# Weighing the values of four attention heads in one block instead of four: exponentials double-buffered by group

## The reference, cut to what matters

```python
Q = (query @ Wq.T + bq)      # per head 128 x 32
K = (key_value @ Wk.T + bk)  # per head 2048 x 32
V = (key_value @ Wv.T + bv)
scores = jnp.einsum('bhqd,bhkd->bhqk', Q, K) / scale
weights = jax.nn.softmax(scores, axis=-1)
attn = jnp.einsum('bhqk,bhkd->bhqd', weights, V)
```

## Time and profile before

| | |
|---|---|
| device time, median of 3 runs | 2168.75 us (2167.66 to 2169.62) |
| the profiled execution, its own time | 2168.71 us |
| its span in the trace | 2166.6 us |
| PE busy in the span | 1995.5 us, 92% |
| DVE, ACT, POOL busy | 1440.0, 858.5, 1177.4 us |
| mean granted clock of PE | 0.959 of full speed |
| attention, first scores to last multiplication | 145.5 to 1240.3 us of the span |

### The profile page before, as it was taken

One profiled execution on the slowest core, in us unless ns is written; L12 is line 12 of the kernel. 1 busy time (PEld: TensorE's weight loads), 2 busy tenths in 40 slices (PEclk: granted clock), 3 DMA queues, 4 the chain that ended last, 5 costly groups with the idle time before them and its releaser, 6 DMA issues. The chain is left out here.

```text
span 2166.6 us, 41731 instructions
## 1 busy us (share of the span) xinstructions
PE 1995.5 (92%) x15544; PEld 1422.7 (66%) x15544; DVE 1440.0 (66%) x1442; ACT 858.5 (40%) x1239; POOL 1177.4 (54%) x837
## 2 busy tenths in 40 slices
PE   6989999999999999999955579989999999899999
PEld 3867777777777777777744338655555554378874
DVE  5126766767676767667665458089999995836555
ACT  1124444444444444444422214276676651133310
POOL 3126667676666766666644431079989993322200
PEclk9999999999999999999975689999999999999999
DMA  4545555555555555555422150040040003001101
GB/s 176 152 137 170 161 178 173 154 179 170 163 168 162 174 174 161 169 166 168 144 87 67 37 182 0 16 104 1 1 117 1 1 16 127 20 6 68 53 1 39
DMA packets 181602, 229.57 MB, mean 106 GB/s; under 512 B 21312, under 2 KB 111936, under 8 KB 175264
## 3 DMA queue, kind: packets, MB, share of 16 engines
q1 hardware_dynamic: 181408, 226.91, 34.0%
HBM read 153.30 MB, written 73.53 MB: 105 GB/s over the span
## 5 line engine op out<-in xcount | busy, mean ns | idle before, releaser
L368 POOL TENSOR_TENSOR a_half<-a_pt 128x1024 f32<-128x1024 f32 x128 | 306.9, 2398 | 373.9 <-ACT a_pt L418 373.9
L418 ACT ACTIVATE a_pt<-a_shift 128x2048 f32<-128x2048 f32 x128 | 245.1, 1915 | 555.7 <-PE a_o L600 460.3
L487 DVE TENSOR_TENSOR a_shift<-a_s,a_neg_rows 128x2048 f32<-128x2048 f32 x128 | 293.3, 2291 | 195.7 <-ACT a_neg_rows L430 195.7
L474 DVE TENSOR_REDUCE a_top<-a_s 128x128 f32<-128x2048 f32 x128 | 293.1, 2290 | 73.7 <-PE a_s L575 73.7
L575 PE MATMUL a_s<-a_q_stack,a_stack 32*128 32x128 f32 x4096 | 163.9, 301 | 48.0 <-DVE a_shift L487 40.2
L575 PEld LDWEIGHTS a_s<-a_q_stack,a_stack 32*128 32x128 f32 x4096 | 138.6, 202 | 93.0 <-DVE a_shift L487 72.8
L534 PE MATMUL a_pj<-p_c_hi,p_wk_hi 128*128 128x512 f32 x448 | 198.5, 443 | 0.0
L963 POOL TENSOR_TENSOR s_even_drive<-s_du,l_rows 128x512 f32<-128x512 f32 x128 | 162.7, 1271 | 64.3 <-DMA s_c_row<-bc_scratch 61.1
L359 POOL TENSOR_TENSOR p_c_lo<-a_raw,p_c_hi 128x512 fp32r<-128x512 f32 x120 | 153.0, 1275 | 73.9 <-ACT p_c_hi L405 73.9
L534 PE MATMUL a_pj<-p_wv_hi,p_c_hi 128*128 128x512 f32 x448 | 185.4, 414 | 0.0
L971 POOL TENSOR_TENSOR s_odd_seen<-s_odd_state,s_c_row 128x512 f32<-128x512 f32 x128 | 162.7, 1271 | 34.0 <-DVE s_odd_state L1102 15.1
(11 more groups left out here) (206 smaller groups left out, 3819.3 us busy)
## 6 DMA issues: line engine op xcount, KB each, us to landing
kv_scratch<-a_k_new SPq DMA_DIRECT2D x128, 256.0 KB, 2.5
kv_scratch<-a_v_new SPq DMA_DIRECT2D x128, 256.0 KB, 3.6
a_stack<-kv_scratch SPq DMA_DIRECT2D x512, 64.0 KB, 2.3
a_v<-kv_scratch SPq DMA_DIRECT2D x32, 1024.0 KB, 6.4
a_raw<-in_ctx SPq DMA_DIRECT2D x120, 256.0 KB, 3.4
a_q_stack<-q_scratch SPq DMA_DIRECT2D x128, 64.0 KB, 2.1
s_c_row<-bc_scratch SPq DMA_DIRECT2D x32, 256.0 KB, 6.0
e_ew_raw<-in_ew SPq DMA_DIRECT2D x8, 1024.0 KB, 4.9
```

What stands on the lines that cost most here:

```text
L368: nc.gpsimd.tensor_tensor(half[:], w[:, 0:2], w[:, 2:4], ALU.add).then_inc(halved, 1)
L418: nc.scalar.activation(pt_head(g, p), shift[:].rearrange("p (i n) -> p i n", n=BANK), ACT.Exp).then_inc(exped, 1)
L474: dve.tensor_reduce(top[:], s_ps[:].rearrange("p i n -> p (i n)").rearrange("p (k q) -> p q k", q=L), AX.X, ALU.max).then_inc(blocked, 1)
L487: dve.tensor_tensor(shift[:].rearrange("p (k q) -> p k q", q=L), s_ps[:].rearrange("p i n -> p (i n)").rearrange("p (k q) -> p k q", q=L), ...
```

## The change

`pt` becomes twice as large, with one half for even and one for odd groups, always head first. The exponentials of group g now wait only until group g - 2 has been weighed and halved (and the first two groups for nothing). PE weighs all four chunks of group g - 1 together in slot 1 of group g, 64 matmuls in a row, and sums the parts in slot 2, by the new function `total`. Slots 0 and 3 weigh nothing. The number of matmuls, their shapes, and all other engines' lists are the same. `finish_group` stays after the shift of slot 3.

```diff
-        pt = st.sb("pt", [P, HG, CH, BANK])
+        pt = st.sb("pt", [P, 2, HG, CH, BANK])
...
-        pt_head = lambda g, p: pt[:, p] if g % 2 == 0 else pt[:, :, p]
-        pt_chunk = lambda g, p, i: pt[:, p, i] if g % 2 == 0 else pt[:, i, p]
+        pt_head = lambda g, p: pt[:, g % 2, p]
+        pt_chunk = lambda g, p, i: pt[:, g % 2, p, i]
...
-                if not (fresh and g == 0):
-                    act.wait_ge(weighed, CH * (GROUPS * b + g - 1) + p + 1)
-                    act.wait_ge(halved, HG * (GROUPS * b + g))
+                if not (fresh and g <= 1):
+                    act.wait_ge(weighed, CH * (GROUPS * b + g - 1))
+                    act.wait_ge(halved, HG * (GROUPS * b + g - 1))
...
-            def weigh(b, g, i, fresh):
+            def weigh(b, g, fresh):
-                if i == 0:
-                    pe.wait_ge(exped, HG * (GROUPS * b + g + 1))
-                    pe.wait_ge(v_in[g % 2], 16 * (GROUPS // 2 * b + g // 2 + 1))
-                    if not (fresh and g == 0):
-                        pe.wait_ge(out_ready, GROUPS * b + g)
-                for j in range(KV):
+                pe.wait_ge(exped, HG * (GROUPS * b + g + 1))
+                pe.wait_ge(v_in[g % 2], 16 * (GROUPS // 2 * b + g // 2 + 1))
+                if not (fresh and g == 0):
+                    pe.wait_ge(out_ready, GROUPS * b + g)
+                for i in range(CH):
+                    for j in range(KV):
...
+                    mm.then_inc(weighed, 1)
+            def total(b, g):
+                pe.wait_ge(parted, HG * (GROUPS * b + g + 1))
...
-                if g >= 1:
-                    weigh(b, g - 1, p, first)
-                elif not first:
-                    weigh(b - 1, GROUPS - 1, p, False)
+                if g >= 1 or not first:
+                    before = (b, g - 1) if g >= 1 else (b - 1, GROUPS - 1)
+                    if p == 1:
+                        weigh(*before, first)
+                    if p == 2:
+                        total(*before)
...
-            for i in range(CH):
-                weigh(B - 1, GROUPS - 1, i, False)
+            weigh(B - 1, GROUPS - 1, False)
+            total(B - 1, GROUPS - 1)
```

More of the change, by code:

```diff
@@ L589, in turn_negative @@
                 pe.transpose(m_ps[:, L:2 * L], neg_wide[:], ident[:]).then_inc(neg_turned, 1)
-            def weigh(b, g, i, fresh):
-                if i == 0:
-                    pe.wait_ge(exped, HG * (GROUPS * b + g + 1))
-                    pe.wait_ge(v_in[g % 2], 16 * (GROUPS // 2 * b + g // 2 + 1))
-                    if not (fresh and g == 0):
-                        pe.wait_ge(out_ready, GROUPS * b + g)
-                for j in range(KV):
-                    for q in range(HG):
[L600 to L610, removed]
@@ new lines, in weigh @@
+            def weigh(b, g, fresh):
[5 more added lines that the diff above has]
+                    for j in range(KV):
+                        for q in range(HG):
+                            mm = pe.matmul(o_ps[DH * q:DH * q + DH, :L], v[:, g % 2, KV * i + j, DH * q:DH * q + DH],
+                                           pt_chunk(g, q, i)[:, j * L:(j + 1) * L], start=(i == 0 and j == 0),
+                                           stop=(i == CH - 1 and j == KV - 1), tile_position=(0, DH * q))
+                    mm.then_inc(weighed, 1)
@@ L612, in _ @@
+            def total(b, g):
+                pe.wait_ge(parted, HG * (GROUPS * b + g + 1))
+                for j in range(2):
+                    for q in range(HG):
+                        mm = pe.matmul(o_ps[DH * q:DH * q + DH, L:2 * L], ones[:, :DH], part[:, g % 2, q, j * L:(j + 1) * L],
+                                       start=(j == 0), stop=(j == 1), tile_position=(0, DH * q))
+                mm.then_inc(totaled, 1)
             pe.wait_ge(small_in, 48)
```

## The result

| | before | changed |
|---|---|---|
| device time, median of 4 runs each | 2169.18 us (2167.66 to 2170.64) | 2232.49 us (2231.87 to 2235.37) |
| ratio of the times, 95% interval | | 1.0295 (1.0277 to 1.0312) |
| span of the profiled execution | 2166.6 us | 2229.8 us |
| batches 1 to 6 | 806.25 us | 862.06 us |
| last batch, first to last scores | 129.83 us | 131.82 us |

A forecast was written before the change was run, and what follows sets the result against it. Each slot was taken as bound by PE's work and the chain over DVE's maxima, balanced within 0.03 us. 27 groups x 2.18 = +58.9, plus +4 in the last batch, on 2168.71 gave 2232 us, range 2221 to 2244.

The forecast's parts named there:

- The floor: Every slot with projections: none can be shorter than about 8.1 us, however little PE has to do in it.
- Slot 0: Loses its weighing but stays at 8.58 us, as DVE's maxima start late: gain 0.
- Slot 2: Loses its weighing, gets the sums (0.55 us); the maxima decide: gain 0.02 us, or 0.18 at most.
- Slot 1: Gets 48 more matmuls between scores and transpose, with no gap to hide them: +2.61 us (2.52 to 2.70).
- Slot 3: Loses weighing and the sums that stuck out, 8.51 to 8.10 us: -0.41 us per group.
- The last batch: No projections, lower clock: earlier exponentials against four bursts of 64 matmuls, together +4 us (0 to +13).
- The relief: Last batch: exponentials no longer wait for the weighing, 14 slots at -0.33 us each, -4.6 us.
- the four blocks: Last batch: four bursts of 64 matmuls, each delaying the transpose from 4.50 to about 7.05 us, +10.2 us.
- the first, PE's total work: Rival: PE's total work sets the pace, so lighter slots shrink and joins save time: 2153 us, chance 0.04.
- The third, that much of the block is covered: Rival: something unseen hides half of slot 1's 2.61 us, -35 us, giving 2197 us; chance 0.04.
- The clock: Rival: idle time in light slots lowers PE's granted clock once per group, +25 us, 2257 us; chance 0.06.
- The rule weighed against the trace: The skill's rule to optimise the busiest engine first implies a gain; the prediction went by the trace's 8.10 us floor instead.

The follow-up runs named there:

- one_chunk_moved: Changed kernel weighing only the first of four chunks in the loop and last batch, but all four in batch 0: 2158.53 us, ratio 0.9955 to the kernel before.
- half_after: Changed kernel with the block maxima taken over only half of the keys: 2149.65 us, ratio 0.9917 to the kernel before.
- pairs: Changed kernel with chunks 0 and 1 weighed in slot 1, 2 and 3 in slot 2, sums in slot 3: 2204.88 us, ratio 1.0157 to the kernel before.
- burst_finish: Changed kernel with a group's reciprocal and multiplication moved before the shift of slot 3: 2224.47 us, ratio 1.0249 to the kernel before.
- spread_early: Changed kernel's double buffer and relaxed waits, but one chunk weighed per slot and sums in slot 3, as before: 2162.88 us, ratio 0.9965 to the kernel before.
- one_chunk: Changed kernel weighing only the first of four chunks everywhere, the others left out of the output: 2176.41 us, ratio 1.0026 to the kernel before.

## Why the prediction was right, step by step

**The floor** (8.1 us for a slot without weighing, from a single kind of slot in batch 0): 8.08 to 8.12 in slot 3 where no jump follows; slot 2 keeps its 0.17 more at the border to slot 3. one_chunk_moved and half_after show that it hangs on DVE's maxima. The prediction's "however little PE has to do in it" is more than any run shows: only work ahead of the transpose was taken away, and in the 4.5 us behind it PE is busy all the time.

**Slot 0**, gain 0 forecast: 8.50 and 8.50. **Slot 2**, gain 0.02: none that can be seen, 8.29 and 8.29.

**Slot 1**, 3 x 0.87 = 2.61 forecast: 2.65 on average. The weighing takes 3.63 from its start to the first key matmul in most groups, that is 3.63 - 1.01 = 2.62 more than one chunk. In group 2 of four batches PE pauses 0.32 to 0.42 us after it with no wait shown, which lifts the average by 0.06.

**Slot 3**, -0.41 forecast in every group: right where no jump follows (8.51 to 8.10), but not in the five slots that pass the loop's jump, 9.31 on average before and 9.34 now. Here a term was mis-sized: the sum had no price for the jump, and PE's idle time behind it was longer in the changed kernel. The first scores after one jump, before and now:

```profile
824.49 0.73 PE L575 MATMUL a_s<-a_q_stack,a_stack 32*128 32x128 f32 x16 [0.78 <-issue]
```

```profile
868.60 0.61 PE L575 MATMUL a_s<-a_q_stack,a_stack 32*128 32x128 f32 x12 [1.02 <-issue]
```

Over the five jumps this idle time is 0.51 to 0.83 us before and 0.66 to 1.92 now. A light slot 3 doesn't bring that by itself: with slot 3 as short, those five slots average 8.99, 8.98 and 8.90 in one_chunk_moved, pairs and burst_finish. Why the changed kernel lost its 0.41 there stays open. It cost 2.2 us against the sum. The groups with projections came to +62.2 (6.83 in batch 0, 55.81 in batches 1 to 6, -0.40 in the last slot of batch 6) instead of +58.9; the rest of the difference is 0.04 in slot 1 of each of the 24 groups, and 0.3 in batch 0.

**The last batch**, +4 forecast: +2.0 between first and last scores, and 0.2 less in its tail. A slot with the block takes 10.9 instead of 9.5, the others 8.75 to 8.96 instead of 8.95 to 9.48 (but for the first, 8.24, as short as before):

```profile
1200.51 2.09 PE L575 MATMUL a_s<-a_q_stack,a_stack 32*128 32x128 f32 x32 [2.68 <-DVE a_shift L487]
...
1202.53 4.79 PE L600 MATMUL a_o<-a_pt,a_v 128*32 128x128 f32 x128
...
1207.25 0.33 PE L583 MATMUL a_m<-a_ident,a_top 128*128 128x128 f32 x1
1207.62 0.29 DVE L481 TENSOR_REDUCE a_neg_max<-a_m 128x1 f32<-128x128 f32 x1 [2.65 <-PE a_m L583]
1207.94 0.40 ACT L424 ACTIVATE a_neg_wide<-a_ones,a_neg_max 128x128 f32<-128x128 f32 x1 [5.54 <-DVE a_neg_max L481]
```

The transpose comes 6.74 into the slot instead of the 7.05 that I took, and the widening follows the negative at once, without the 0.5 us that ACT lost in the earlier trace rows. The relief that I put at 4.6 us is 6.1 in spread_early, which has nothing else. With that, the four blocks cost 2.0 + 6.1 = 8.1 where the sum had 10.2. So the mechanism was right, and both terms were off a little, both making the forecast too high here.

Added up: 62.2 + 2.0 - 0.2 = 64.0, and the stages after attention took 0.8 us less in this execution, which gives the 63.2 between the two spans. An error of 3 us with projections and one of 2 us in the last batch cancelled, and that the forecast met the median to half a microsecond is luck; the range of 23 us was the honest width. Of the **rivals**, the first, PE's total work, is refuted by one_chunk_moved; it comes near only where the maxima are short, in half_after. The third, that much of the block is covered, is refuted by the 10.76 of slot 1. The clock stayed at 1.00 in batches 1 to 6 of the changed kernel, with 1.3 us of idle time in slot 0 and once 1.92 behind a jump. It fell with the pauses of 2.7 to 2.9 us in one_chunk and after the 2.38 of half_after, so the danger was real, but not with the gaps that the change makes.

**The rule weighed against the trace** came out as the trace had it. The Trainium skill, "Perfetto Trace Analysis", § Identifying the Most-Contended Engine, would have had us relieve PE, the busiest engine. Its warning that the busy share of matmuls is a poor measure doesn't change that: the weight loads, by which it goes instead, were busy for 614.83 us of batches 1 to 6, more than DVE's 558.10. The trace disagrees for the part of PE's work that was tried: PE was busy 99% of batches 1 to 6, and a quarter fewer matmuls there bought 1.2%.

## What to carry to other kernels

Where two engines meet at one semaphore in each step of a pipeline, what counts is each step's own maximum of both, not the sum of either over the loop: fill every step evenly up to the chain beside it, and don't gather work in one. An engine's long wait (460 us on ACT here) says nothing until one finds what ends after it; removing it alone was worth 6 us, moving 1.2 us of DVE work per group into a gap that DVE already had was worth 13. To ask whether an order matters, shorten the chain beside it and compare both orders.

## What had not been expected of the hardware

A loop's jump costs PE a varying time. From the last matmul of an iteration to the first scores of the next there are 0.78 and 1.02 us of idle time in the rows above, and the same slots differ by up to 1.3 us within one execution (8.83 to 10.10 in the changed kernel). A kernel can also have a pause of 2.7 to 2.9 us in the middle of a row of matmuls at each pass, and the same loop behind other code can be free of it: 18 us between one_chunk and one_chunk_moved, although the latter does 144 matmuls more. One pair shows this, and its cause isn't shown. A difference of under 1% between two kernels whose code has another length should be looked at for such pauses before it is put down to the change.
